# Graph network and mixture-of-experts layer on one core: a second DMA queue at the layer border, and one-hot tables interleaved by two

## What is computed

```python
def _sage_conv(x, edge_index, W_l, W_r, b):
    src, dst = (edge_index[0], edge_index[1])
    agg_sum = jax.ops.segment_sum(x[src], dst, num_segments=x.shape[0])
    deg = jax.ops.segment_sum(jnp.ones((edge_index.shape[1],), x.dtype), dst, num_segments=x.shape[0])
    return (agg_sum / jnp.maximum(deg, 1.0)[:, None]) @ W_l + x @ W_r + b

h = jax.nn.relu(_sage_conv(_layernorm(x), edges, W1_l, W1_r, b1))
x = x + _sage_conv(h, edges, W2_l, W2_r, b2)
tokens = _layernorm(x)
probs = jax.nn.softmax(tokens @ router_w.T)        # the two best of 8 experts, weights normed to 1
# out = tokens + sum over the two experts of weight * (gelu(tokens @ w1[e] + b1[e]) @ w2[e] + b2[e])
x = x + out
```

## Time and profile before

| what | value |
|---|---|
| median of 3 runs | 811.55 us (810.81 to 812.03) |
| the profiled execution's own time | 810.48 us |
| its span in the profile | 808.8 us |
| PE busy | 635.0 us (79%) |
| DVE busy | 421.0 us (52%) |
| ACT, POOL busy | 208.4 us, 209.2 us (26% each) |
| granted TensorE clock, mean | 0.907 of full speed |

### The profile page before, as it was taken

One profiled execution on the slowest core, in us unless ns is written; L12 is line 12 of the kernel. 1 busy time (PEld: TensorE's weight loads), 2 busy tenths in 40 slices (PEclk: granted clock), 3 DMA queues, 4 the chain that ended last, 5 costly groups with the idle time before them and its releaser, 6 DMA issues.

```text
span 808.8 us, 14181 instructions
## 1 busy us (share of the span) xinstructions
PE 635.0 (79%) x3239; PEld 371.1 (46%) x3240; DVE 421.0 (52%) x1256; ACT 208.4 (26%) x447; POOL 209.2 (26%) x261
## 2 busy tenths in 40 slices
PE   1359999998799999999979999998079999992000
PEld 1135656665344444444434544444056777772000
DVE  3699899998232233223236566667823333332443
ACT  0017777877211111111101000000123434440000
POOL 4703223222000000000000434343602222225774
PEclk9859999999799999999989999999579999997555
DMA  3101111111111111111521366532333333334774
GB/s 101 39 7 39 39 52 39 40 51 33 54 41 58 58 51 46 58 58 52 189 56 56 112 213 210 189 111 95 127 119 102 101 102 100 101 99 137 205 204 137
DMA packets 68102, 74.47 MB, mean 92 GB/s; under 512 B 11071, under 2 KB 62916, under 8 KB 68078
## 3 DMA queue, kind: packets, MB, share of 16 engines
q1 hardware_dynamic: 59150, 52.69, 21.2%
q0 software_dynamic: 8352, 20.96, 8.2%
q10 hardware_dynamic: 576, 0.52, 0.2%
HBM read 42.65 MB, written 31.49 MB: 92 GB/s over the span
## 4 chain that ended last, share of the span: by engine, by line
PE 49%; issue 14%; DVE 11%; DMA 10%; POOL 7%; ACT 4%; SPq 1%; DVEq 1%; ACTq 1%; POOLq 0%
PE counts_ps L1182 20%; PE bank L1138 9%; PE counts_ps L1329 7%; PE bank L1346 6%; PE counts_ps L592 3%; DMA y<-ys_dram,adj 3%; ACT adj L599 3%; DVE onehots L579 3%; POOL xs_dram L531 2%; POOL y L562 2%; POOL adj L501 2%; DMA xs_dram<-onehots 2%; DMA xs_dram<-w,onehots 2%; PE bank L1337 2%; PE counts_ps L1313 2%
## 5 line engine op out<-in xcount | busy, mean ns | idle before, releaser
L1182 PE MATMUL counts_ps<-y,adj 128*128 128x512 f16 x1250 | 290.6, 382 | 7.1 <-DMA onehots<-in_L_ffn_router_w 5.2
L1182 PEld LDWEIGHTS counts_ps<-y,adj 128*128 128x128 f16 (+1 forms) x1250 | 122.5, 100 | 149.8 <-issue 18.6
L1138 PE MATMUL bank<-w,rows 128*128 128x512 f32 x200 | 105.5, 632 | 2.1 <-ACT rows L1374 0.8
L592 PE MATMUL counts_ps<-onehots 125*128 125x100 f16 x784 | 89.3, 272 | 13.5 <-DVE onehots L579 11.3
L592 PEld LDWEIGHTS counts_ps<-onehots 125*128 125x128 f16 x784 | 69.0, 118 | 57.4 <-DVE onehots L579 39.3
L599 ACT ACTIVATE adj<-counts_ps 128x800 f32 (+1 forms) x98 | 80.7, 836 | 31.9 <-PE counts_ps L592 29.4
L579 DVE TENSOR_TENSOR onehots<-iota,lo_t 125x1024 f16<-125x1024 f16 x98 | 67.3, 687 | 2.6 <-PE counts_ps L592 1.1
L1329 PE MATMUL counts_ps<-adj 128*128 x224 | 57.3, 400 | 2.8 <-ACT adj L1456 1.6
L554 POOL DMA_DIRECT2D ys_dram<-adj x52 | 28.2, 542 | 121.1 <-DVE adj L1045 114.6
L1037 DVE TENSOR_TENSOR adj<-counts_ps,adj 128x256 f32<-128x256 f32 x54 | 22.9, 425 | 66.3 <-PE counts_ps L1329 66.3
L816 DVE TENSOR_TENSOR rows<-rows,b1b 128x256 f32<-128x256 f32 x25 | 10.6, 425 | 87.9 <-DMA rows<-z_dram 87.9
(11 more groups left out here) (210 smaller groups left out, 669.9 us busy)
## 6 DMA issues: line engine op xcount, KB each, us to landing
adj<-xs_dram SPq DMA_DIRECT2D x56, 128.0 KB, 2.1
ys_dram<-adj POOLq DMA_DIRECT2D x52, 128.0 KB, 2.0
z_dram<-zt SPq DMA_DIRECT2D x50, 128.0 KB, 1.8
rows<-z_dram SPq DMA_DIRECT2D x50, 128.0 KB, 2.1
rows<-in_x SPq DMA_DIRECT2D x48, 128.0 KB
adj<-in_L_ffn_w SPq DMA_DIRECT2D x16, 256.0 KB, 3.4
u_dram<-yo SPq DMA_DIRECT2D x25, 128.0 KB, 1.9
y<-u_dram SPq DMA_DIRECT2D x25, 128.0 KB, 2.9
```

What stands on the lines that cost most here:

```text
L592: last = nc.tensor.matmul(counts_ps[:, 2 * slot + g, h * P:h * P + KEYS], stat_g[:, :, h:h + 1].rearrange("p k a -> p (k a)"), mov_g[:, :, ...
L1138: last = te.matmul(bank[1][:, :], nrm_t[:, k * P:(k + 1) * P], w[:, k, :], start=(k == 0), stop=(k == KD - 1))
L1182: last = te.matmul(sums[:, s, :], adj[:, b, bass.ds(t * P, P)], y[:, b, :], start=(b == 0), stop=(b == NT - 1))
```

## The change

Three things are changed together. The computation stays the same.

1. DMA issues move from SP's queue to ACT's: the router's weights (now at the start of `phase2`, ahead of the first `turn`), the stores of the last two `z2` tiles, and the first `zi` load of layer 2. The load of `xt` for layer 2 stays on SP but stands before `phase2`.
2. The last `z2` tile is written to `uo` (the memory of `yo`) in place of `zt`, and DVE's wait for the first store goes.
3. `HALF` goes from 4 to 2: the one-hot tables are interleaved by two windows, 4 bytes from one element of a window to its next. The count banks keep their layout through `OF_BANK` = 4. The `iota_4` table is half as long.

```diff
-    HALF = 4
+    HALF = 2
+    OF_BANK = 4
...
+            sp.dma_start(xt[:, :], x[0:P, :]).then_inc(S["x_in"], 16)
+
             def root_rows(t):
...
-            sp.dma_start(xt[:, :], x[0:P, :]).then_inc(S["x_in"], 16)
-            for t in range(NT - DIRECT, NT):
-                sp.wait_ge(S["yz_in"], t + 1 + NT)
-                sp.dma_start(z2_dram[t * P:(t + 1) * P, :], zt[:, :]).then_inc(S["z2_last"], 16)
-            sp.wait_ge(S["h_in"], NT)
-            sp.dma_start(zi[:, :], z2_dram[0:P, :]).then_inc(S["z_in"], 16)
             sp.wait_ge(S["z2_last"], 16 * DIRECT)
-            for k in range(KD):
-                sp.dma_start(rw_t[:, k, :], router_w[:, k * P:(k + 1) * P].rearrange("e p -> p e")
-                             ).then_inc(S["rw_in"], 16)
...
-                    oh[0:RUN, slot, :].rearrange("p (g k w) -> p g k w", g=2, w=HALF),
-                    iota_4[0:RUN, 0:n, :].rearrange("p (g k) w -> p g k w", g=1).to_broadcast((RUN, 2, n, HALF)),
+                    oh[0:RUN, slot, :].rearrange("p (g k w) -> p g k w", k=n, w=HALF),
+                    iota_4[0:RUN, 0:n, :].rearrange("p (g k) w -> p g k w", g=1).to_broadcast((RUN, GW // HALF, n, HALF)),
...
-            for g in range(2):
+            for g in range(GW // HALF):
...
-                    last = nc.tensor.matmul(counts_ps[:, 2 * slot + g, h * P:h * P + KEYS],
+                    bank_of, at = divmod(g * HALF + h, OF_BANK)
+                    last = nc.tensor.matmul(counts_ps[:, 2 * slot + bank_of, at * P:at * P + KEYS],
...
-            for t in range(NT - DIRECT, NT):
-
-                dve.wait_ge(S["y2_out"], 32 * (NT - DIRECT))
-                if t > NT - DIRECT:
-                    dve.wait_ge(S["z2_last"], 16 * (t - NT + DIRECT))
-                split_y(t + NT, yrow(t), s2, b2b[:, :])
+            dve.wait_ge(S["y2_out"], 32 * (NT - DIRECT))
+            for t, root_to in zip(range(NT - DIRECT, NT), (zt[:, :], uo)):
+                split_y(t + NT, yrow(t), s2, b2b[:, :], root_to)
...
+            for k in range(KD):
+                act.dma_start(rw_t[:, k, :], router_w[:, k * P:(k + 1) * P].rearrange("e p -> p e")
+                              ).then_inc(S["rw_in"], 16)
+
...
                 turn(t + NT, ACT.Relu)
                 high(t + NT, y[:, t, D:2 * D], scl_i[:, 9:10].bitcast(F32))
+                act.wait_ge(S["yz_in"], t + 1 + NT)
+                act.dma_start(z2_dram[t * P:(t + 1) * P, :], zt[:, :] if t < NT - 1 else uo).then_inc(S["z2_last"], 16)
+            act.wait_ge(S["y2_out"], 32 * (NT - DIRECT))
+            act.wait_ge(S["h_in"], NT)
+            act.dma_start(zi[:, :], z2_dram[0:P, :]).then_inc(S["z_in"], 16)
```

More of the change, by code:

```diff
@@ L63, in build @@
     assert max(IN_BATCH) <= BATCH and FIRST_OF[-1] + BATCH <= NB * BATCH
-    assert NW == NG * WPP and N <= NW * WD <= AC and KEYS <= P and GW == 2 * HALF and HALF * P == 512
+    assert NW == NG * WPP and N <= NW * WD <= AC and KEYS <= P and GW == 2 * OF_BANK and OF_BANK % HALF == 0 and OF_BANK * P == 512
     with ExitStack() as ctx:
@@ L579, in group_onehots_now @@
                 last = nc.vector.tensor_tensor(
-                    oh[0:RUN, slot, :].rearrange("p (g k w) -> p g k w", g=2, w=HALF),
-                    iota_4[0:RUN, 0:n, :].rearrange("p (g k) w -> p g k w", g=1).to_broadcast((RUN, 2, n, HALF)),
-                    of[0:RUN, bass.ds(group * GW, GW)].rearrange("p (g a w) -> p g a w", g=2, a=1
-                                                                 ).to_broadcast((RUN, 2, n, HALF)), ALU.is_equal)
+                    oh[0:RUN, slot, :].rearrange("p (g k w) -> p g k w", k=n, w=HALF),
+                    iota_4[0:RUN, 0:n, :].rearrange("p (g k) w -> p g k w", g=1).to_broadcast((RUN, GW // HALF, n, HALF)),
+                    of[0:RUN, bass.ds(group * GW, GW)].rearrange("p (g a w) -> p g a w", a=1, w=HALF
+                                                                 ).to_broadcast((RUN, GW // HALF, n, HALF)), ALU.is_equal)
             last.then_inc(S["onehot"], 1)
@@ L600, in group_keep @@
                 adj[:, :, bass.ds(group * GW * WD, GW * WD)].rearrange("p b (h d) -> p b h d", d=WD),
-                counts_ps[:, 2 * slot:2 * slot + 2, :].rearrange("p g (w c) -> p (g w) c", w=HALF)[:, :, 0:KEYS]
+                counts_ps[:, 2 * slot:2 * slot + 2, :].rearrange("p g (w c) -> p (g w) c", w=OF_BANK)[:, :, 0:KEYS]
                 .rearrange("p h (b d) -> p b h d", d=WD),
@@ L709, in stats, with split_y @@
                 v.tensor_scalar(stat[:, 9:10], stat[:, 7:8], EPS, None, ALU.add).then_inc(S["var_in"], 1)
-            def split_y(t, out_, scale, bias=None):
+            def split_y(t, out_, scale, bias=None, root_to=zt[:, :]):
                 dve.wait_ge(S["hi_in"], t + 1)
@@ L715, in split_y @@
                 if bias is not None:
-                    last = v.tensor_tensor(zt[:, :], bank[1][:, D:2 * D], bias, ALU.add)
+                    last = v.tensor_tensor(root_to, bank[1][:, D:2 * D], bias, ALU.add)
                 last.then_inc(S["yz_in"], 1)
```

## The result

| | before | after |
|---|---|---|
| median | 811.25 us (810.81 to 812.03) | 801.30 us (798.91 to 803.33) |
| profiled execution; its span | 810.48; 808.8 us | 800.83; 799.1 us |
| mean granted clock of TensorE | 0.907 | 0.907 |

A forecast was written before the change was run, and what follows sets the result against it. The prediction took waits at the layer border as the main bound, then layer 1's nearly full DVE and its aggregation's start. Its terms -8.2 + 0.8 - 1.6 = -9.0 us gave 802.5 us against the median of 811.55, range 799.0 to 807.3.

The forecast's parts named there:

- Border, -8.2: Layer border: without PE's waits and the half clock, the first token's transposes begin at 410.3 instead of 418.51, saving 8.2 us.
- The store's landing: Border: the z2 store shares the DMA engines with the chunk loads instead of standing behind them, costing at most 0.5 us.
- rival D: Border: stores on the second queue are still served behind the chunk loads; 803.5 us, chance 0.05.
- Router's loads, +0.8: Start of layer 1's aggregation: the router's weights delay the zi load and PE, costing 0.8 us (0 to 1.5).
- Front, -1.6: Layer 1's front: one-hots by two shorten PE's 8 pairs to about 0.65 us, saving 1.6 us (4.0 at best).
- Layer 2, 0: Behind the border: PE sets the pace, so the shift goes through to the end, with no further gain or loss.
- A: Layer 1's front: PE's pairs don't get shorter and the front stays as it is; 804.1 us, chance 0.22.
- B: Border: the clock falls all the same, so the border is worth 5.7 us; 805.0 us, chance 0.08.
- C: Front: DVE's rate falls with rows of two, 0.98 us more a group if element cost doubles; 900 us, chance 0.09.

## Why the prediction was right, point by point

- **Border, -8.2: right in size** (197.75 to 189.59 is 8.16) and in what it is made of: no wait of PE from 398 us on, the clock at 1.00, the second tile directly behind the first. The share of each edit was left open by it. The runs give 6.8 to the place of the router's loads and the other 1.4 to 1.8 to the own buffer with the masks behind it, together with the `xt` load, which no run separates from it.
- **The store's landing: wrong, without effect.** I let the store share the DMA engines with the chunks for at most 0.5 us. It took 6.2, so the store is as late as in rival D. Its price didn't come, because the `zi` load doesn't wait for the stores: it went out at 399.92, where the forecast's 402.7 less the 3.1 us by which all is earlier is 399.6; the chunks had all but landed, and it took 2.5 us, where 2.4 were reckoned with. DVE had its rows at 402.44.
- **Router's loads, +0.8: right.** +0.9 in the trace; 12.8 to 13.2 in all traces without them there, 13.7 to 14.0 in all with them.
- **Front, -1.6: the mis-sized term**, in the sentence "I take 1.6". The pair fell to 0.068 us and not 0.08, and the tile to 5.77 or 5.78, below the 5.86 that was taken as its bound: from the statistics to the norming it is 115.91 - 113.04 = 2.87 us now, where 2.97 was the better of two readings from a trace in which PE was still late. By that (5.98 - 5.78) x 22 = 4.4 us were to be had. The forecast had given 4.0 as the best case and then taken less than half, for no reason that a row carried. What the clock took back, 1.4 us a fall (7.23 and 7.12 against 5.77), I had not seen as something the edit could change. With it the 22 tiles gave 2.3 us in the first trace; the other 1.7 of the 4.0 lie ahead of them and behind them, where the forecast had counted nothing. In the mean of the seven traces by two against the four by four it is 2.8 in the 22 tiles and 3.5 up to the front's last transposes. The net is -4.0 in the first trace, -3.2 between otherwise equal kernels.
- **Layer 2, 0: the missing step.** "The shift goes through to the end" holds for PE's own pace, but SP's loads of rows stand behind the experts' weights, two loads of 256 KB and their biases for a tile, and how long DVE and then PE wait varies between traces (PE's longest wait there is 1.25 to 2.23 us in the ten traces with the loads on SP, and the clock fell behind it in two). The rows of it (a wait of 3.59 us on DVE and 1.64 on PE) were in the trace of before, and I had not read that stretch. Moved to ACT's queue, the loads leave PE 0.9 us of wait at every such place.
- **Rivals.** A fell: by the rule of two hits on a 16-byte line (Trainium skill, "Advanced Engine Details and Errata", Memory Cachelines) 4 bytes would bring nothing over 8, and the rows show 0.91 and 0.54. B fell: the clock stayed at 1.00 through the border. C's condition didn't hold for rows of two (0.69 and 0.57 us as before); for rows of one its price did: 0.94 us more for a group against the 0.98 worked out, and 890.0 us against 900.

That the sum was nearer than its parts is luck: the front gave 2.4 us more than forecast and layer 2 lost 2.3, and neither knew of the other.

## What to carry to other kernels

When a table of 16-bit elements is written by DVE and read by TensorE with a stride, interleave by two: DVE keeps its rate with rows of two, and 4 bytes was the widest distance tried at which 8 pairs took their least time (0.54 us). A transfer that seems to be stuck in a queue may be held by the bytes in flight: here moving it to another queue brought nothing (6.2 us against 6.6), but an own buffer for who waits for it, or an issue at a quieter time, did. Where loads share a queue, look whether those needed in some microseconds stand behind those needed in a hundred (0.3 to 2.9 us here); and read the trace at every place behind the edit where a wait is already near to being critical.

## What the runs showed of the hardware

- 128 KB from a second queue took 6.2 us to land beside the chunk loads of 2.9 MB, against 6.6 behind them on the same queue; their first packet moved 4.0 us after the issue.
- Two loads of 4 KB each, element by element, lengthened DVE's wait for the row load beside them by 0.6 to 0.9 us (3.84 with them, 3.22 and 2.97 without).
- The granted clock fell to 0.50 in the front, where PE had been busy for 1.36 of the 2 us before with no wait over 0.6 us near it; and it fell after PE's wait of 2.12 us in layer 2 in one trace, but not after 1.86, nor after 2.03 and 2.23 in two others, while it did after 1.91 in one. How long PE stood still doesn't tell it.
- A pair that repeats the window of the pair before it took 0.046 us ((0.77 - 0.54) / 5), against 0.068 for pairs over different windows.
